# Attention with left-out tiles and a mixture of experts on one core: keys taken relative to the mean of 16 keys, and a smaller norm bound in the rule for left-out tiles

## What is computed

```python
q = _lora(x, Wq, Aq, Bq).reshape(B, T, H, dh).transpose(0, 2, 1, 3)     # k and v alike
s = jnp.einsum('bhqd,bhkd->bhqk', q, k) / jnp.sqrt(jnp.float32(dh))
bias = slopes[:, None, None] * (i - j).astype(jnp.float32)              # slopes 2^(-(h+1)/2)
s = s + bias[None]
s = jnp.where(j[None, None] <= i[None, None], s, NEG_INF)
out = jnp.einsum('bhqk,bhkd->bhqd', jax.nn.softmax(s, axis=-1), v)
x = _layernorm(x + out.transpose(0, 2, 1, 3).reshape(B, T, E) @ Wp.T)
x = _layernorm(x + moe(x))          # 8 experts, top 2, capacity 1076
```

## Time and profile before

| | |
|---|---|
| runs | 1310.98, 1310.62, 1307.44 us |
| median | 1310.62 us |
| the profiled execution | 1314.12 us, of which the span from first to last instruction is 1312.4 us |
| its start, up to the first exp of a turn | 40.03 us |
| its turns, from the first exp to the last copy of `ps_o` | 40.03 to 835.73 us |
| busy over the span | PE 89%, ACT 70%, DVE 48%, POOL 27% |

### The profile page before, as it was taken

One profiled execution on the slowest core, in us unless ns is written; L12 is line 12 of the kernel. 1 busy time (PEld: TensorE's weight loads), 2 busy tenths in 40 slices (PEclk: granted clock), 3 DMA queues, 4 the chain that ended last, 5 costly groups with the idle time before them and its releaser, 6 DMA issues. The chain is left out here.

```text
span 1312.4 us, 24491 instructions
## 1 busy us (share of the span) xinstructions
PE 1162.6 (89%) x8759; PEld 495.6 (38%) x8759; DVE 633.8 (48%) x1767; ACT 919.0 (70%) x1203; POOL 354.6 (27%) x382
## 2 busy tenths in 40 slices
PE   7899999999999998999898889516999999999990
PEld 4322222222222222221222111114877877777770
DVE  4534342232546253625252301264687677677756
ACT  2799999999999897988798989215354354445414
POOL 2422112020131312312131300033535534544430
PEclk9999999999999998999898979857999999999995
DMA  6942422223231221213120100335135333422216
GB/s 152 195 104 67 94 67 70 58 73 100 60 107 53 94 66 44 78 49 89 36 81 9 38 3 7 122 106 173 22 108 125 49 98 107 92 45 29 27 21 256
DMA packets 83745, 104.22 MB, mean 79 GB/s; under 512 B 14937, under 2 KB 68932, under 8 KB 83632
## 3 DMA queue, kind: packets, MB, share of 16 engines
q1 hardware_dynamic: 66512, 77.74, 21.0%
q0 software_dynamic: 15744, 23.83, 8.7%
q10 hardware_dynamic: 1376, 1.18, 0.7%
HBM read 56.99 MB, written 48.29 MB: 80 GB/s over the span
## 5 line engine op out<-in xcount | busy, mean ns | idle before, releaser
L1358 ACT ACTIVATE prob<-ps_s 128x1024 f32<-128x1024 f32 (+3 forms) x854 | 719.3, 972 | 73.8 <-PE ps_s L1259 62.9
L1276 PE MATMUL ps_o<-prob,v_aug 128*17 128x512 f32 (+3 forms) x3294 | 436.2, 577 | 7.6 <-POOL prob L1384 2.9
L1259 PE MATMUL ps_s<-qop,kop 51*128 51x512 f16 (+3 forms) x1647 | 269.3, 374 | 39.6 <-ACT prob L1358 27.1
L1259 PEld LDWEIGHTS ps_s<-qop,kop 51*128 51x128 f16 x1647 | 63.1, 93 | 419.8 <-ACT prob L1358 381.9
L2109 PE MATMUL ps_y<-w2s,hs 128*128 128x256 bf16 (+1 forms) x1728 | 189.1, 273 | 1.1 <-DVE yb L2194 1.1
L2090 PE MATMUL ps_h<-xs,w1s 128*128 128x384 bf16 (+1 forms) x1152 | 181.7, 317 | 5.0 <-ACT hid L2156 4.3
L1384 POOL TENSOR_SCALAR_AFFINE_SELECT prob<-prob 128x256 f32<-128x256 f32 (+1 forms) x180 | 69.5, 397 | 418.2 <-ACT prob L1358 415.7
L2156 ACT ACTIVATE hid<-ps_h,b 128x384 f32<-128x384 f32 (+1 forms) x192 | 105.1, 560 | 109.9 <-PE ps_h L2090 86.0
L1420 DVE COPY acc<-ps_o 32x512 f32<-32x512 f32 (+2 forms) x105 | 72.1, 687 | 220.5 <-PE ps_o L1276 204.3
L2109 PEld LDWEIGHTS ps_y<-w2s,hs 128*128 128x128 bf16 (+1 forms) x1728 | 157.6, 99 | 18.3 <-DVE yb L2194 1.5
L2047 POOL DMA_INDIRECT result<-y,entry x72 | 111.7, 1551 | 175.7 <-DVE y L2199 142.1
(11 more groups left out here) (163 smaller groups left out, 731.7 us busy)
## 6 DMA issues: line engine op xcount, KB each, us to landing
w<-in_W SPq DMA_DIRECT2D x16, 1024.0 KB, 7.5
slots_x<-empty POOLq DMA_DIRECT2D x12, 520.0 KB, 4.1
qop<-fparts_q SPq DMA_DIRECT2D x42, 128.0 KB, 4.2
xe<-slots_x SPq DMA_DIRECT2D x8, 650.0 KB
x_all<-in_xT SPq DMA_DIRECT2D x8, 512.0 KB, 4.8
attnT<-acc SPq DMA_DIRECT2D x128, 32.0 KB
aT<-attnT SPq DMA_DIRECT2D x16, 256.0 KB
x_all<-in_x SPq DMA_DIRECT2D x8, 512.0 KB
```

The costliest lines, as they stand in the source:

```text
L1259: mm = pe.matmul(ps_s[:, u.p % SLOTS_S, e, a.q0:], o.key(e, a.h, a.kt), o.query(e, a.h, a.b, a.q0), start=True, stop=True)
L1276: mm = pe.matmul(ps_o[32 * c:32 * c + VW, a.q0:], o.v[:, a.kt, a.h], prob[:, t % RING, c % 2, c // 2, a.q0:], start=a.first, stop=a.last)
L1358: act.activation(prob[:, t % RING, n, e:z, q0:], ps_s[:, u.p % SLOTS_S, e:z, q0:], ACT.Exp, scale=1.0 / (SCALE * SCALE)).then_inc(exp_done, 1)
```

## The change

`BOUND` goes from 76 to 55, and `key_tiles` now counts the distance from the middle of the first 16 keys (7.5 keys more), so `TILES` becomes [2, 3, 4, 6, 8, 10, 15, 20, 29, 32 and so on]. The plan built from it has 1618 tiles, 841 exps, 409 turns and 102 jobs of evicting, in place of 1647, 854, 417 and 99. `dve_less` takes the mean of the first 16 keys in place of the first key, in two instructions in place of one. The tables of the pieces' turns are written anew; from `HALF_AT[4]` on nearly all numbers differ. The key rows of block 5 need one pair of heads less. The diff, with one line of the tables:

```diff
-BOUND = 76.0
+BOUND = 55.0
+ANCHOR = 16
 UNDER = BOUND + 104.0
-    return min(T // P, math.ceil(UNDER / slope / P))
+    return min(T // P, math.ceil((UNDER / slope + (ANCHOR - 1) / 2) / P))
...
-COUNT_AT = {0: 186, 1: 216, 2: 250, 3: 276, 4: 310, 5: 337, 6: 368}
-SETUP_TURN, BOUND_TURN = 76, 341
+COUNT_AT = {0: 182, 1: 210, 2: 246, 3: 269, 4: 307, 5: 332, 6: 363}
+SETUP_TURN, BOUND_TURN = 76, 338
...
         if m >= 2:
-            act.wait_ge(j.less_set, m - 1)
+            act.wait_ge(j.less_set, 2 * (m - 1))
...
     def dve_less(j, dve, k, bank):
         dve.wait_ge(j.proj_mm, k + 1)
-        dve.tensor_scalar(j.less[:, TILE_ORDER[k] - 2], bank[:, 0:1], -1.0, None, ALU.mult).then_inc(j.less_set, 1)
+        less = j.less[:, TILE_ORDER[k] - 2]
+        dve.tensor_reduce(less, bank[:, 0:ANCHOR], AX.X, ALU.add).then_inc(j.less_set, 1)
+        dve.wait_ge(j.less_set, 2 * k + 1)
+        dve.tensor_scalar(less, less, -1.0 / ANCHOR, None, ALU.mult).then_inc(j.less_set, 1)
```

More of the change, by code:

```diff
@@ L219 @@
            3: (45, 47, 50, 54, 57, 59, 62, 66),
[4 rows of a table removed]
[L224 to L237, removed]
-COUNT_AT = {0: 186, 1: 216, 2: 250, 3: 276, 4: 310, 5: 337, 6: 368}
-SETUP_TURN, BOUND_TURN = 76, 341
[4 rows of a table added]
+NORM_AT = {2: 28, 3: 68, 4: 115, 5: 168, 6: 235, 7: 305}
+VALUE_AT = {2: (30, 34, 38, 42),
+            3: (71, 74, 82, 84),
+            4: (119, 122, 129, 131),
+            5: (176, 178, 180, 189),
+            6: (240, 244, 250, 260),
+            7: (309, 323, 327, 335)}
+ROUTE_AT = {0: (157, 162, 166, 170),
+            1: (186, 191, 195, 197),
+            2: (219, 222, 230, 233),
+            3: (248, 252, 254, 257),
+            4: (279, 281, 287, 290),
+            5: (314, 316, 318, 320),
+            6: (341, 343, 345, 350)}
+COUNT_AT = {0: 182, 1: 210, 2: 246, 3: 269, 4: 307, 5: 332, 6: 363}
+SETUP_TURN, BOUND_TURN = 76, 338
 PIECE_AT = {SETUP_TURN: ("setup",), BOUND_TURN: ("bound",)}
```

## The result

| | before | with the change |
|---|---|---|
| median | 1311.26 us (8 runs, 1307.44 to 1315.85) | 1302.16 us (8 runs, 1297.14 to 1307.03) |
| ratio | | 0.9925, 95% interval 0.9902 to 0.9948 |
| the profiled execution | 1314.12 us, span 1312.4 | 1307.03 us, span 1305.2 |

The change is faster by 9.1 us. The forecast was 14.5 us and a time of 1296.1; the measured 1302.16 lies 6.1 above it, inside the range of 1284 to 1308.

What follows compares the result with a forecast made beforehand. The prediction took ACT's exps to bound the turns, with PE close behind. Its terms, -11.7 - 0.8 - 2.0 + 0 + 0 = -14.5 us, took the median of 1310.62 to 1296.1 us, range 1284 to 1308.

Steps and rivals of the forecast that it cites:

- rival 1: Scatters in the turns: cheap sets become dear, 5.7 us each, taking the gain back (1313 to 1317); chance 0.10.
- The exps: ACT in the turns: fewer exps, counted by form from the two plans, save 11.7 us.
- The masks: POOL at block 6's diagonal: split moves out, ACT's wait of 2.72 goes; -2.0 us, bounds -2.7 to +2.
- Tail and pieces: One-tile turns ending the plan: two fewer waits, -0.8 us; value and routing pieces among the turns: 0, bounds -2 to +2.
- The start: Before the first exps: two-instruction `less` comes some 0.25 us later but is covered; cost 0, at most 0.5.
- What does not move: Block 5's key loads and everything after the turns, experts included: instructions and data stay, so no change in time.
- Rival 2: Scatters in the turns: two or three dear sets become cheap, -11.4 to -17.2 us, giving 1285 to 1279; chance 0.13.
- Rival 3: Last two thirds of the turns: pieces, not exps, set the pace; saving only 6.7 us, so 1304; chance 0.14.
- Rival 4: Norm-product flag: if set, the general program runs, over 1700 us on top; chance under 1 in 100.

Runs made afterwards that it cites:

- e1: The changed kernel run again, unchanged, on a low chip: 1267.37 us against 1279.61 for the kernel before, ratio 0.9904.
- e4: The changed kernel with the old tables of the pieces' turns, on a low chip: 1277.41 us, ratio 0.9983 to the kernel before.
- e10: The changed kernel with 184 never-executed PE increments and scatters paced two turns apart by exps, high chip: 1265.22 us against 1310.33 before, ratio 0.9647.
- e9: The changed kernel with 184 never-executed PE increments that move the code behind them, high chip: 1296.19 us against 1310.33 for the kernel before, ratio 0.9890.
- e2: The kernel before with only the 16-key mean as reference key, on a low chip: 1278.95 us against 1279.61, ratio 1.0003.
- e8: The changed kernel with one of each block's eight scatters kept in the turns, high chip: 1268.96 us against 1313.76 for the kernel before.

## Why the prediction was right, and where it was not

The time lies in the range, and the terms for the turns were right in mechanism and sum. The step that failed is "What follows the turns keeps its instructions and its data", which put the experts at 0. With the stall's 2.8 us in it the sum would have said 11.7; 12.2 was measured on a low chip and 9.1 in the first pair, whose interval (some 7 to 13 us) holds 11.7. What is left to the 9.1 is near what high chips charged the new plan beyond the old (2.8 us of idle time, under rival 1): 15.1 in the turns of the low chip, less 2.8, less 2.8, is 9.5. Of these two misses the prediction knew only the second, as a rival; the time stayed in the range because the range was made wide for the scatters, and that it covered the stall too is luck.

**The exps: right.** -11.7 forecast; -12.0 in the first pair, -11.6 on the low chip.

**The masks: right, by the row chosen.** ACT behind block 6's diagonal, and POOL ahead of it, in the change:

```profile
554.41 0.79 POOL L1389 TENSOR_SCALAR_AFFINE_SELECT prob<-prob 128x256 f32<-128x256 f32 x2
555.37 1.00 POOL L1839 DMA_INDIRECT slots_x<-xsplit,dest_all  x1 [0.17 <-issue]
...
556.61 1.94 ACT L1363 ACTIVATE prob<-ps_s 128x1024 f32<-128x1024 f32 x2 [1.05 <-PE ps_s L1264]
```

The wait is 1.05 us, as in the earlier trace rows, in place of 2.72. Turns 260 to 280 are 2.1 us shorter with the new tables than with the old (36.3 in e1, 38.4 in e4). What I did not see is that this set would be the only cheap one on a high chip: its 12 turns took some 3 us more than the exps in them (0.905 us for 1024 elements from start to start, shorter ones in proportion to their rows), those of the other six 5 to 10. The masks had spaced its first scatters some 2 us apart; that this is what made it cheap is argued, and e10 agrees.

**Tail and pieces: right as a sum, wrong as a picture.** With masks and tail the idle time was to fall by 2.8; it fell by 4.2 on the low chip, within the bounds of the pieces, and by 1.4 in the first pair. (By the plans the turns at the end with one tile in each unit, or in one unit alone, are 9 before and 7 after, not 12 and 10; the difference of two is right.) But I put the tables at nothing because they held the same pieces in 8 turns less. The run with the old tables says that the new ones are worth 10 us against those on a low chip. The pairs of pieces that I counted say nothing about which DVE copy of `ps_o` falls behind which routing step, and e4 shows what that costs: 3.88 us in one place.

**The start: right.** Ratio 1.0003.

**What does not move: wrong, and the failing step.** "What follows the turns keeps its instructions and its data" is true, but its instructions lie elsewhere. Fewer turns bring PE's loop over the experts forward, by 184 instructions in my count, across an edge behind which it is no longer kept between passes. Price: 2.7 to 2.8 us in each profile of the change, and 5.3 in the first one with what followed there (1.3 us for 3.4 us at 1.2 GHz, and 1.2 us in two other experts, which executions without the stall show too). With the code moved back the gain was 14.1 us (interval 10 to 19); the sum said 14.5.

**Rival 1: the mechanism real, the sign open as I had left it.** Dense scatters cost the change 31.5 us on a high chip (turns of 779.2 us against 747.7 paced, e9 and e10). For before it is argued: 795.7 in the first pair against 762.2 paced on a low chip. The change moved the dear places but hardly their sum: what high chips add to the exps' idle time is 29.0 us for the old plan (73.8 less 44.8) and 31.8 for the new (72.4 less 40.6). The prediction's count of three cheap sets was off: its stretch of 560 to 600 us holds only the end of one (POOL busy 2.29 in the earlier trace rows). That set ran from 552.2 to 562.2 us, and its 12 turns took 4.5 us over their exps, against 1.0 in e2 on a low chip. **Rival 2** was within reach, though not by these tables. **Rival 3** falls: on the low chip, the tiles and tables brought 15.1 us in the turns. **Rival 4** did not come: the 841 exps are those of the program without the flag.

The Trainium skill (SBUF — State Buffer, Who interferes with whom) states that a DMA never contends with a compute engine. The runs e8 and e10 speak against using that as a rule for a schedule on these high chips: fewer or slower scatters, with the matmuls unchanged, gave PE and ACT 31 to 33 us back. They don't show by which path.

## What to carry to other kernels

- Read a stage that the change doesn't touch all the same: when code ahead of a loop gets shorter, compare the packets of PE's instruction queue and look for a wait with no releaser at the head of a pass (2.5 to 5.4 us here). Padding inside a branch that is not taken moves code for nothing.
- A table of turns paces an engine only where that engine waits for something in each turn. Give indirect DMAs beside a PE-bound stretch a wait of their own, and look at their spacing in the timeline.
- Tables fitted to one plan are part of that plan: change the plan and fit them again, or the gain may be gone (10 of 12 us on a low chip).

## What the runs showed of the hardware

**PE's results can come later than its records say.** On a high chip, in a dense set, the piece of four matmuls starts at 501.50 and DVE gets its result only at 505.45. On a low chip the same piece starts at 491.20 and DVE starts at 492.40. The change on the high chip, then on the low:

```profile
501.50 1.16 PE L599 MATMUL ps_r<-x_all 128*128 128x264 f32 x4
...
505.45 0.42 DVE L741 COPY v_aug<-ps_r 128x256 f32<-128x256 f32 x1 [2.93 <-remote]
```

```profile
491.20 1.16 PE L599 MATMUL ps_r<-x_all 128*128 128x264 f32 x4
...
492.40 0.43 DVE L741 COPY v_aug<-ps_r 128x256 f32<-128x256 f32 x1 [0.18 <-PE ps_r L599]
```

The matmul records look the same in both, the consumers don't. The semaphore that this piece increments moves at 505.43 in the first trace and at 492.37 in the second, just ahead of DVE each time. So "idle without a cause" behind a matmul can be PE, or the way of its results, held up. What holds it, the rows written or the making of the descriptors, and why some chips show it and others not, stays open.

**PE's instruction memory.** A packet of q8 is 1.08 MB / 66 = 16 KB. By my count, a loop of 1705 instructions is run twice without a new fetch when it begins at place 12 of its block of 256, and is fetched again when it begins at 84, 142 or 210, with 2.5 to 5.4 us of stall. The Trainium skill (Advanced Engine Details and Errata, ISA Cache) gives 128 KB for TensorE in lines of 16 KB or 256 instructions. By that, 7 such lines fit with one to spare and 8 fill it. The traces agree with the size of the packet. A loop of 7 lines that is kept speaks against the page's remark that there are only 2 lines; that one of 8, which should just fit, is fetched again is left open, and so is the one at place 84.
